# The last stage as one phase: output projection, routing and chosen experts by chunks of 128 tokens

## The chip, the cores and the metric

The kernel runs on one core of one Trainium2 chip. The metric is the device time of one execution in microseconds. The core has five engines, each with its own instruction stream, which wait for one another by semaphores: TensorE (PE in the rows, its weight loads PEld), VectorE (DVE), ScalarE (ACT), GpSimd (POOL) and SyncE (SP, which here only issues DMA transfers). All numbers are float32; a float32 matmul of 128x512 shows as two PE instructions, so "x32" in a row of the trace is 16 matmuls of the code.

## The reference

Four sequences ("batches") of 512 tokens, 512 features wide, pass through four sublayers, each as `x = x + layernorm(f(layernorm(x)))`. The change touches the end of the third (its projection with `Wo` and the two layer norms) and the whole of the fourth:

```python
    return o @ Wo                                    # end of the third sublayer
...
    x0 = x[:, :ROUTE_LEN].reshape(b, -1)             # all 512 x 512 values of a batch
    logits = x0 @ switch_w.T + switch_b              # 8 numbers for a batch
    probs = jax.nn.softmax(logits, axis=-1)
    gate, top_idx = jax.lax.top_k(probs, TOPK)       # 2 experts for a batch
    xh = x.reshape(b, s, H, DH).transpose(0, 2, 1, 3)
    w1s, b1s = (w1[top_idx], b1[top_idx])
    w2s, b2s = (w2[top_idx], b2[top_idx])
    h = jnp.einsum('bhsd,bkfd->bkhsf', xh, w1s) + b1s[:, :, None, None, :]
    h = jax.nn.gelu(h, approximate=False)
    o = jnp.einsum('bkhsf,bkdf->bkhsd', h, w2s) + b2s[:, :, None, None, :]
    o = (o * gate[:, :, None, None, None]).sum(axis=1)
    out = x + o
    return out @ w3.T + b3
```

The experts of a batch can be chosen only when all of its 512 tokens have left the layer norm. The choice concerns that batch alone.

## The kernel before

The kernel is a row of phases; the last two are `phase_delta_out` (tiles named `d_`) and `phase_experts` (tiles named `e_`). The phases ahead of them are the same in both kernels.

`phase_delta_out` works on a batch at a time, four chunks of 128 tokens in each. Per chunk TensorE does 16 matmuls (`outputs`, L2270), one for each head, into one of two PSUM tiles `yo`; ScalarE copies the tile to `y` (L2285), and GpSimd issues the load of the heads for the same chunk of the next batch (L2259). When the four chunks of a batch are there, VectorE normalises them together (`norm_y_vector`, L140 to L154), adds them to `x`, normalises the sum (`norm_x_vector`, L161 to L169), and multiplies the normalised batch with the router's weights for each of the 8 experts (L2312, 2048 columns each, summed by the instruction). ScalarE supplies the inverse square roots by Ln and Exp (L176 to L186), each after a load of its table. TensorE turns the normalised batch (`norm_x_tensor`, L202, 16 transposes) into `XT`, after the outputs of the next batch; for the last batch there is nothing ahead of it.

`phase_experts` begins when `phase_delta_out` has ended on all engines. One matmul sums the routers' parts over the partitions (L2385). VectorE does softmax and the top two for all four batches (L2434 to L2441), picks the chosen experts' weights for all four (`choose`, L2449 and L2451; `choose_bias`, L2456 and L2458), and then a loop runs over the batches: the chosen weights are laid on a block diagonal (L2475), TensorE does hidden layers (L2391) and output layers (L2398) for four groups of features, ScalarE does Gelu between them (L2425), VectorE adds the input (`e_mixed`, L2478), TensorE does the last layer for four chunks (L2412), VectorE adds its bias (L2482), and `norm_y_vector` normalises and adds the batch to `x`, which SP stores (L133).

What sets the order is the order in which each engine's code is written, and the waits; there is no scheduler. The block diagonal of a batch (L2475) stands on VectorE behind the closing norm of the batch ahead.

## Time and profile before

| | us |
|---|---|
| median of 3 runs | 3439.75 (3439.09 to 3444.64) |
| the profiled execution | 3439.55 |
| its span, first to last instruction | 3437.9 |
| first matmul of `phase_delta_out`, from the span's start | 2948.49 |
| PE busy, share of the span | 3019.9, 88% |
| DVE busy | 1859.0, 54% |
| ACT busy | 1200.4, 35% |

In such a profile an engine's busy share is an average over all stages. The two phases of the change are the last 490 us of the span, and are to be read by stretches of time. "PEclk" is the granted TensorE clock, 1.00 for 2.4 GHz and 0.50 for 1.2 GHz. A row of a timeline gives the start, the length, the engine, the line, and in brackets how long the engine was idle before it and what it waited for.

### The profile page before, as it was taken

How to read it: one execution, taken by the hardware profiler on the slowest of the kernel's cores; microseconds unless marked ns; L12 is line 12 of the kernel's file. 1: busy time of each engine (PE TensorE's matmuls, PEld its weight loads, DVE VectorE, ACT ScalarE, POOL GpSimd, SP SyncE). 2: the span in 40 equal slices, each digit the busy share in tenths (PEclk: the TensorE clock that was granted, in tenths of full speed). 3: DMA queues.
4: the chain of work that ended last, by engine and by line, in shares of the span. 5: the costliest groups of instructions: out<-in, count | busy, mean ns of one | idle time of the engine just before them, and what ended most of it. 6: DMA issues, size and time to landing. Idle time of an engine off the chain costs nothing. (4 is left out here: it accounts for less than half of the span.)

```text
span 3437.9 us, 42357 instructions
## 1 busy us (share of the span) xinstructions
PE 3019.9 (88%) x13268; PEld 1724.8 (50%) x13269; DVE 1859.0 (54%) x4426; ACT 1200.4 (35%) x2133; POOL 637.7 (19%) x775
## 2 busy tenths in 40 slices
PE   7899969989996789999999999999999985799276
PEld 3344444435663446665556665566555664344122
DVE  5766730001111867767777677776677764064533
ACT  3554310102211544444544445443454433011121
POOL 1111113001112111222312223122222223000000
PEclk9999969999998889999999999999999997899588
DMA  3001150022123510010000110001100000631111
GB/s 111 25 13 37 61 211 13 24 98 66 62 67 135 224 61 13 14 63 35 17 26 13 63 38 17 23 13 63 38 20 20 13 13 19 250 122 61 43 41 45
DMA packets 67801, 196.98 MB, mean 57 GB/s; under 512 B 10512, under 2 KB 11168, under 8 KB 61216
## 3 DMA queue, kind: packets, MB, share of 16 engines
q1 hardware_dynamic: 46080, 142.06, 11.1%
q0 software_dynamic: 11168, 35.70, 3.1%
q10 hardware_dynamic: 10368, 16.83, 1.3%
q8 instruction: 107, 1.75, 0.2%
q14 instruction: 78, 0.64, 0.1%
HBM read 137.90 MB, written 56.66 MB: 57 GB/s over the span
## 5 line engine op out<-in xcount | busy, mean ns | idle before, releaser
L2061 DVE SCALAR_TENSOR_TENSOR c_conv<-c_ps_pj,c_conv_t,c_conv 128x511 f32<-128x511 f32 (+2 forms) x495 | 368.9, 745 | 35.8 <-ACT c_conv L1910 24.1
L2270 PE MATMUL d_ps_yo<-d_w_o,d_heads 128*128 128x512 f32 x512 | 226.0, 604 | 23.7 <-DMA d_heads<-ot_d 23.7
L1701 PE MATMUL c_ps_pj<-c_xs,c_w_v 128*128 128x512 f32 x480 | 240.8, 626 | 0.0
L1716 PE MATMUL c_ps_pj<-c_w_g,c_xs 128*128 128x512 f32 x512 | 227.6, 592 | 0.0
L1701 PE MATMUL c_ps_pj<-c_xs,c_w_k 128*128 128x512 f32 x480 | 217.7, 597 | 1.9 <-DMA c_xs<-xt_d 1.9
L1701 PE MATMUL c_ps_pj<-c_xs,c_w_q 128*128 128x512 f32 x360 | 166.4, 606 | 25.8 <-DVE c_conv L2061 24.9
L2270 PEld LDWEIGHTS d_ps_yo<-d_w_o,d_heads 128*128 128x128 f32 x512 | 99.1, 194 | 148.9 <-issue 148.9
L1910 ACT ACTIVATE c_conv<-c_ps_pj,c_conv_t 128x512 f32<-128x512 f32 x165 | 127.8, 775 | 116.6 <-PE c_ps_pj L1701 108.8
L1716 PEld LDWEIGHTS c_ps_pj<-c_w_g,c_xs 128*128 128x128 f32 x512 | 94.8, 190 | 107.1 <-issue 107.1
L2082 DVE TENSOR_TENSOR c_block_X<-c_block_X,c_block_t 128x126 f32<-128x126 f32 (+22 forms) x496 | 137.5, 277 | 18.8 <-DVE c_block_t L2078 2.0
L2078 DVE TENSOR_TENSOR c_block_t<-c_block_L,c_block_X 128x126 f32<-128x126 f32 (+22 forms) x496 | 137.0, 276 | 17.5 <-DVE c_block_X L2082 1.7
L1113 DVE TENSOR_TENSOR x_act<-x_hs,x_ps_u 128x352 f32<-128x352 f32 x40 | 20.8, 521 | 227.0 <-ACT x_hs L1098 227.0
L1744 PE MATMUL c_ps_kk<-c_kT 128*128 128x128 f32 x512 | 105.4, 289 | 35.9 <-DVE XT L2153 25.6
L1701 PEld LDWEIGHTS c_ps_pj<-c_xs,c_w_k 128*128 128x128 f32 x480 | 87.1, 191 | 89.3 <-issue 87.2
L1637 POOL TENSOR_TENSOR XT<-XT,c_ln_w 128x512 f32<-128x512 f32 x64 | 81.3, 1270 | 253.4 <-DVE c_block_L L2084 221.2
L966 DVE TENSOR_TENSOR b_act<-b_hs,b_ps_u 128x512 f32<-128x512 f32 (+1 forms) x24 | 16.5, 686 | 206.3 <-PE b_ps_u L858 206.3
L1960 ACT ACTIVATE c_err<-c_negL 32x128 f32<-32x128 f32 x256 | 78.6, 307 | 135.6 <-DVE c_negL L2151 130.9
L1064 PE MATMUL x_ps_g<-b_w_gu,x_xT 128*128 x320 | 122.7, 465 | 1.4 <-ACT x_xT L1089 0.8
L377 PE MATMUL a_ps_pj<-XT,a_w_in 128*128 128x512 f32 x256 | 120.7, 616 | 3.5 <-DVE a_conv L602 2.7
L1701 PEld LDWEIGHTS c_ps_pj<-c_xs,c_w_q 128*128 128x128 f32 x360 | 65.4, 191 | 115.9 <-issue 66.2
L1065 PE MATMUL x_ps_u<-b_w_gu,x_xT 128*128 x320 | 122.0, 463 | 0.0
L357 POOL TENSOR_SCALAR a_skip<-a_xc,a_col_d 128x512 f32<-128x512 f32 x32 | 62.6, 1958 | 315.5 <-ACT a_xc L471 173.0
(377 smaller groups left out, 6116.9 us busy)
## 6 DMA issues: line engine op xcount, KB each, us to landing
c_xs<-xt_d SPq DMA_DIRECT2D x16, 1024.0 KB, 4.9
ot_d<-c_oT ACTq DMA_DIRECT2D x64, 256.0 KB, 2.0
d_heads<-ot_d POOLq DMA_DIRECT2D x16, 1024.0 KB, 7.1
b_w_gu<-in_w_gu SPq DMA_DIRECT2D x8, 1408.0 KB, 25.4
y_slots<-x_y SPq DMA_DIRECT2D x40, 256.0 KB, 2.0
a_x<-in_x SPq DMA_DIRECT2D x8, 1024.0 KB, 6.7
x_w_dn<-in_w_dn SPq DMA_DIRECT2D x8, 768.0 KB, 11.0
x<-a_x SPq DMA_DIRECT2D x4, 1024.0 KB, 4.3
```

The costliest lines, as they stand in the source:

```text
L377: mm = e.matmul(pj[c % 2][:, :], w_in[:, k, c * P:(c + 1) * P], XT[:, b, k, :], start=(k == 0), stop=(k == KD - 1))
L1064: e.matmul(g_ps[par][:, 0:FE], xT[par][:, k, :], w_gu[:, expert, k, 0:FE], start=(k == 0), stop=(k == KD - 1))
L1065: mm = e.matmul(u_ps[par][:, 0:FE], xT[par][:, k, :], w_gu[:, expert, k, FE:2 * FE], start=(k == 0), stop=(k == KD - 1))
L1637: e.tensor_tensor(o[:, c], o[:, c], b, op).then_inc(o_gated, 1)
L1701: mm = e.matmul(bank_of[u][:, :], w["kqv"[u // HG]][:, k, (u % HG) * DH:(u % HG + 1) * DH], xs[xb][:, k, :], start=(k == 0), stop=(k == KD ...
L1716: mm = e.matmul(pj[1 - i % 2][:, :], xs[xb][:, k, i * P:(i + 1) * P], w["g"][:, k, :], start=(k == 0), stop=(k == KD - 1))
L1744: e.matmul(kk[:, h, :], chunk(kT, h, c), chunk(kT, h, c), start=True, stop=True)
L1910: e.activation(conv[:, u % 4, :], bank_of[u][:, :], ACT.Identity, bias=conv_t[buf][:, m, h, TAPS:TAPS + 1], scale=conv_t[buf][:, m, h, TAP ...
L2061: e.scalar_tensor_tensor(oc, bank_of[u][:, 0:SEQ - s], conv_t[buf][:, m, h, TAPS - 1 - s:TAPS - s], oc, ALU.mult, ALU.add).then_inc(conv_s ...
L2078: e.tensor_tensor(t, block_L[:, i + 1:BB, i].unsqueeze(2).to_broadcast([P, n, k]), block_X[:, i, 0:k].unsqueeze(1).to_broadcast([P, n, k]) ...
L2082: e.tensor_tensor(below, below, t, ALU.add).then_inc(sub_step, 1)
L2270: mm = e.matmul(yo[c % 2][:, :], heads[:, c, h, :], w_o[:, h, :], start=(h == 0), stop=(h == NH - 1))
```

## The change

The two phases become one, `phase_out` (all its tiles are named `d_`). The batch is no longer the unit of the norms and the router: every chunk of 128 tokens is normalised as soon as its 16 matmuls are done, by ScalarE straight from PSUM (`scale`), turned one chunk later (`turn`), and multiplied with its 512 columns of the router's weights (`switch_part`, four experts before and four after the second norm of the next chunk). Each batch is routed in the chunks of the next one (`route_front`, `route_back`, `choose`), the experts of batch 0 stand within the matmuls of chunk 14 (`EARLY`), and those of batch 1 behind the last layer of batch 0. The last norm takes its inverse root from VectorE (`last_root`, 16 small steps) in place of Ln and Exp, and ScalarE does its scaling (`scale_z`). All heads are loaded from SP's queue, `w_o` and the router's weights in four parts each. ScalarE's tables are loaded by hand, five changes of table after the first. The loops over batches are written out.

```diff
+ROUTE_FRONT, ROUTE_BACK, ROUTE_STEPS = 4, 20, 35
+Z_STEPS = 16
...
-def phase_delta_out(pr, con, XT, route_part):
+def phase_out(pr, con, XT):
...
+        z = [yn[0], xn[0], yn[1], xn[1]]
...
+        z_ps = [yo[0], yo[1], o_ps[0], o_ps[1]]
...
+            load_heads(0)
+            for g in range(NG):
+                e.dma_start(w_o[:, g * HG:(g + 1) * HG, :], io["w_o"][:, g * HG:(g + 1) * HG, :]).then_inc(wo_loaded[g], 16)
+            load_heads(1)
+            for c in range(TPB):
+                load_x(c)
...
+            load_switch(0)
+            load_switch(1)
+            for n in range(NT):
+                if n + 2 < NT:
+                    load_heads(n + 2)
+                if n == 0:
+                    load_switch(2)
+                    load_switch(3)
+                    e.dma_start(w3[:, :, :], io["w3"]).then_inc(w3_loaded, 16)
+                store_x(n)
+                if n > 0 and n + TPB - 1 < NT:
+                    load_x(n + TPB - 1)
...
+            def outputs(n, of=range(NH)):
+                if of[0] == 0:
+                    e.wait_ge(heads_loaded[n % 2], 16 * (n // 2 + 1))
+                    if n >= 2:
...
+            def turn(n):
+                e.wait_ge(x_normed, n + 1)
+                if n >= 1:
+                    e.wait_ge(xt_done, n)
+                for k in range(KD):
+                    mm = e.transpose(turned[:, k, :], xn[n % 2][:, k * P:(k + 1) * P], con["ident"][:, :])
+                mm.then_inc(turn_ready, 1)
...
+            def output_layer(b, dc):
+                m = KD * b + dc
+                if m >= 2:
+                    e.wait_ge(mixed_done, m - 1)
+                if b > 0 and dc < 2:
+                    e.wait_ge(z_added, TPB * (b - 1) + dc + 3)
...
+            def chosen_experts(b):
                 e.wait_ge(diag_done, 4 * b + 4)
-                hidden_layer(0)
+                e.wait_ge(xt_done, TPB * (b + 1))
...
+            def last_layer(b):
+                e.wait_ge(w3_loaded, 16)
+                for c in range(TPB):
+                    if b == 0 and c < 2:
+                        e.wait_ge(y_normed, NT - 1 + c)
+                    elif c < 2:
+                        e.wait_ge(z_added, TPB * (b - 1) + c + 1)
...
+            for n in range(NT):
+                if n == EARLY:
+                    outputs(n, range(SPLIT))
+                    chosen_experts(0)
+                    outputs(n, range(SPLIT, NH))
+                else:
+                    outputs(n)
+                if n > 0:
+                    turn(n - 1)
+                if n % TPB == 1 and n > TPB:
+                    route_logits(n // TPB - 1)
+            last_layer(0)
+            turn(NT - 1)
+            chosen_experts(1)
+            route_logits(NB - 1)
+            last_layer(1)
+            for b in range(2, NB):
+                chosen_experts(b)
+                last_layer(b)
...
+            def scale(n, dst, src, means, mv, ln_done, ln, rstd, rs, offset, nb, normed):
+                e.wait_ge(means, n + 1)
+                e.activation(ln[:, :], mv[:, 1:2], ACT.Ln, bias=con["eps"][:, :]).then_inc(ln_done, 1)
+                e.wait_ge(ln_done, n + 1)
+                e.activation(rs[:, :], ln[:, :], ACT.Exp, scale=-0.5).then_inc(rstd, 1)
+                e.wait_ge(rstd, n + 1)
+                e.wait_ge(offset, n + 1)
+                e.activation(dst, src, ACT.Identity, bias=nb[:, 0:1], scale=rs[:, 0:1]).then_inc(normed, 1)
...
+            e.preload_act_table_set("natural_log_exp_and_others")
+            for n in range(NT):
+                if n == EARLY:
+                    e.preload_act_table_set("gelu_and_others")
+                    gelus(0)
+                    e.preload_act_table_set("natural_log_exp_and_others")
+                if n > 0:
+                    take_turned(n - 1)
+                scale_y(n)
+                scale_x(n)
+                if n % TPB == 1 and n > TPB:
+                    exponentials(n // TPB - 1)
+            take_turned(NT - 1)
+            e.preload_act_table_set("gelu_and_others")
+            gelus(1)
+            scale_z(0)
+            e.preload_act_table_set("natural_log_exp_and_others")
+            exponentials(NB - 1)
+            e.preload_act_table_set("gelu_and_others")
+            for b in range(2, NB):
+                gelus(b)
+                scale_z(b - 1)
+            scale_z(NB - 1)
...
+                for v in of:
+                    if NE * n + v > 0:
+                        e.wait_ge(switched, NE * n + v)
+                    e.scalar_tensor_tensor(product[:, :], xn[n % 2][:, :], 1.0, switch[:, v, c * DM:(c + 1) * DM],
+                                           ALU.mult, ALU.mult, accum_out=part[b % 2][:, v, c:c + 1]).then_inc(switched, 1)
+            def chunk(n):
+                e.wait_ge(yo_ready, n + 1)
+                statistics(n, yo[n % 2][:, :], y_stats, y_st, y_means, y_mv)
+                if n > 0:
+                    switch_part(n - 1, range(NE // 2))
+                shift(n, y_mv, y_rstd, y_rs, y_offset, y_nb)
+                e.wait_ge(x_loaded[n % TPB], 16 * (n // TPB + 1))
+                e.wait_ge(y_normed, n + 1)
+                xc = x[n % TPB][:, :]
+                e.tensor_tensor(xc, xc, yn[n % 2][:, :], ALU.add).then_inc(x_new, 1)
+                e.wait_ge(x_new, n + 1)
+                statistics(n, xc, x_stats, x_st, x_means, x_mv)
+                if n > 0:
+                    switch_part(n - 1, range(NE // 2, NE))
+                shift(n, x_mv, x_rstd, x_rs, x_offset, x_nb)
...
+            def last_norm(b, c):
+                m = TPB * b + c
+                e.wait_ge(z_ready, m + 1)
+                if b > 0:
+                    e.wait_ge(out_done, m - TPB + 1)
+                e.tensor_tensor(z[c][:, :], z_ps[c][:, :], b3[:, :], ALU.add).then_inc(z_added, 1)
+                e.wait_ge(z_added, m + 1)
+                e.bn_stats(z_st[:, c, :], z[c][:, :]).then_inc(z_stats, 1)
+                e.wait_ge(z_stats, m + 1)
+                e.bn_aggr(z_mv[:, c, :], z_st[:, c, :]).then_inc(z_means, 1)
+            def last_root(b):
+                m = Z_STEPS * b
+                e.wait_ge(z_means, TPB * (b + 1))
+                rstd_vector(e, z_ve[:, :], z_t[:, :], z_rs[:, :], z_mv[:, :, 1], z_step, m)
+                e.wait_ge(z_step, m + Z_STEPS - 1)
+                e.scalar_tensor_tensor(z_nb[:, :], z_mv[:, :, 0], -1.0, z_rs[:, :], ALU.mult, ALU.mult).then_inc(z_step, 1)
+            def finish(b):
+                for c in range(TPB):
+                    m = TPB * b + c
+                    e.wait_ge(x_loaded[c], 16 * (NB + b + 1))
+                    e.wait_ge(z_normed, m + 1)
+                    e.tensor_tensor(x[c][:, :], x[c][:, :], z[c][:, :], ALU.add).then_inc(out_done, 1)
+            for n in range(NT):
+                if n == EARLY:
+                    mix(0)
+                chunk(n)
+                b = n // TPB - 1
+                if b >= 0 and n % TPB == 1:
+                    route_front(b)
+                elif b >= 0 and n % TPB == 2:
+                    route_back(b)
+                elif b >= 0 and n % TPB == 3 and n < NT - 1:
+                    choose(b)
+            e.wait_ge(turn_ready, NT - 1)
+            last_norm(0, 0)
+            last_norm(0, 1)
+            switch_part(NT - 1, range(NE))
+            e.wait_ge(turn_ready, NT)
+            last_norm(0, 2)
+            last_norm(0, 3)
+            last_root(0)
+            choose(NB - 2)
+            mix(1)
+            finish(0)
+            route_front(NB - 1)
+            for b in range(1, NB):
+                for c in range(TPB):
+                    last_norm(b, c)
+                last_root(b)
+                if b == 1:
+                    route_back(NB - 1)
+                if b + 1 < NB:
+                    mix(b + 1)
+                if b == 1:
+                    choose(NB - 1)
+                finish(b)
...
-        phase_delta_out(pr, con, XT, route_part)
-        phase_experts(pr, con, XT, route_part)
+        phase_out(pr, con, XT)```

On TensorE, before, this is what stands between the last outputs and the first expert matmul (`d_ps_tp` the turned chunks, `e_ps_logits` the router's sums, `e_ps_h` the hidden layer):

```order
L202 MATMUL d_ps_tp<-ident,d_yn 128x128 x16
L2219 UNCONDITIONAL_BRANCH
L2382 UNCONDITIONAL_BRANCH
L2385 MATMUL e_ps_logits<-route_part,ones 128x32
L2387 UNCONDITIONAL_BRANCH
L2387 ISA
L2390 ISA
L2391 ISA
L2391 MATMUL e_ps_h<-XT,e_w_diag 128x512
```

Now, on TensorE, from the end of the first batch's experts, which stand within chunk 14 behind 12 of its 16 outputs (`d_ps_o` their output layers, `d_ps_yo` the outputs, L2303 the last layer):

```order
L2278 MATMUL d_ps_o0<-d_hidden,d_w2_diag0 128x512 x2
L2278 MATMUL d_ps_o1<-d_hidden,d_w2_diag0 128x512 x2
L2244 MATMUL d_ps_yo0<-d_w_o,d_heads0 128x512 x4
L2253 MATMUL d_ps_tp<-ident,d_xn1 128x128 x4
L2244 MATMUL d_ps_yo1<-d_w_o,d_heads1 128x512 x16
L2253 MATMUL d_ps_tp<-ident,d_xn0 128x128 x4
L2303 MATMUL d_ps_yo0<-d_w3,d_mixed 128x512 x4
L2303 MATMUL d_ps_yo1<-d_w3,d_mixed 128x512 x4
L2303 MATMUL d_ps_o0<-d_w3,d_mixed 128x512 x4
L2303 MATMUL d_ps_o1<-d_w3,d_mixed 128x512 x4
L2253 MATMUL d_ps_tp<-ident,d_xn1 128x128 x4
L2267 MATMUL d_ps_h0<-XT,d_w1_diag1 128x512
```

The branches between phases are gone, experts and last layer stand among the outputs of the last chunks, and 4 transposes follow every 16 outputs in place of 16 after 64.

On VectorE, before, a batch's norm and the first of its 8 products with the router's weights:

```order
L149 TENSOR_SCALAR d_yn<-d_y,d_mv,d_rs 128x512 x4
L151 ISA
L154 TENSOR_TENSOR d_x<-d_x,d_yn 128x512 x4
L161 BN_STATS d_st<-d_x 128x6 x4
L165 BN_AGGR d_mv<-d_st 128x2 x4
L169 TENSOR_SCALAR d_yn<-d_x,d_mv,d_rs 128x512 x4
L2311 ISA
L2312 SCALAR_TENSOR_TENSOR d_products,d_part<-d_yn,d_switch 128x2048
```

Now, on VectorE, one chunk:

```order
L2398 BN_STATS d_y_st<-d_ps_yo 128x6
L2400 BN_AGGR d_y_mv<-d_y_st 128x2
L2417 SCALAR_TENSOR_TENSOR d_product,d_part<-d_xn,d_switch 128x512 x4
L2404 SCALAR_TENSOR_TENSOR d_y_nb<-d_y_mv,d_y_rs 128x1
L2429 TENSOR_TENSOR d_x<-d_x,d_yn 128x512
L2398 BN_STATS d_x_st<-d_x 128x6
L2400 BN_AGGR d_x_mv<-d_x_st 128x2
L2417 SCALAR_TENSOR_TENSOR d_product,d_part<-d_xn,d_switch 128x512 x4
L2404 SCALAR_TENSOR_TENSOR d_x_nb<-d_x_mv,d_x_rs 128x1
```

The scalings have moved to ScalarE, and the products with the router's weights stand, four at a time, in the gaps in which ScalarE makes a chunk's inverse root.

On VectorE, now, the end of the choice for batch 2 and what follows it, behind chunk 15 (before, the choices of all batches stood ahead of the first block diagonal, L2475):

```order
L2483 TENSOR_TENSOR d_r_score<-d_r_key,d_r_rest 128x8
L2473 TENSOR_TENSOR d_chosen<-d_b,d_r_score 128x8
L2475 TENSOR_REDUCE d_b_sel<-d_chosen 128x1
L2492 TENSOR_TENSOR d_w_diag<-d_same_head,d_w_sel 128x128 x4
L2497 SCALAR_TENSOR_TENSOR d_mixed<-d_ps_o,d_b_sel,XT 128x512 x4
L2523 TENSOR_TENSOR d_x<-d_x,d_yn 128x512
L2523 TENSOR_TENSOR d_x<-d_x,d_xn 128x512
```

The mixing of batch 1 (`d_mixed`), for which TensorE's output layers wait, stands behind the choice for batch 2.

## Rows read from the trace of the kernel before

**Rows 1.** Busy time by stretch: us, PE, PEld, DVE, ACT, POOL, PEclk, DMA share, GB/s

```profile
2948.00:3008.00 60.00, 59.51 (x132) 26.27 (x133) 2.72 (x5) 3.04 (x5) 2.83 (x4) 0.94 0.66 259
...
3128.00:3190.00 62.00, 58.91 (x143) 26.24 (x142) 30.51 (x45) 10.47 (x16) 0.00 (x0) 0.97 0.09 34
3190.00:3220.00 30.00, 4.38 (x16) 2.87 (x16) 24.24 (x33) 8.77 (x13) 0.00 (x0) 0.50 0.09 35
...
3240.00:3271.00 31.00, 11.76 (x23) 4.89 (x24) 17.71 (x59) 5.32 (x8) 0.00 (x0) 0.65 0.00 0
...
3315.00:3355.00 40.00, 27.76 (x55) 11.24 (x54) 12.47 (x27) 8.36 (x11) 0.00 (x0) 0.79 0.16 52
```

**Rows 2.** Timeline of PE: start us, us, engine, line, what, [idle before, releaser]

```profile
2948.49 62.06 PE L2270 MATMUL d_ps_yo<-d_w_o,d_heads 128*128 128x512 f32 x137 [23.67 <-DMA d_heads<-ot_d]
...
3062.94 0.63 PE L202 MATMUL d_ps_tp<-ident,d_yn 128*128 128x128 f32 x4 [0.87 <-ACT XT L193]
...
3203.00 1.12 PE L202 MATMUL d_ps_tp<-ident,d_yn 128*128 128x128 f32 x4 [13.48 <-DVE d_yn L169]
...
3258.48 3.62 PE L2391 MATMUL e_ps_h<-XT,e_w_diag 128*128 x4 [34.12 <-DVE e_w_diag L2475]
...
3300.78 3.78 PE L2391 MATMUL e_ps_h<-XT,e_w_diag 128*128 x4 [10.69 <-DVE e_w_diag L2475]
...
3409.41 14.00 PE L2412 MATMUL e_ps_y<-e_w,e_mixed 128*128 128x512 f32 x32 [0.95 <-DVE e_mixed L2478]
```

**Rows 3.** Timeline of ACT, copies of the first two chunks out of PSUM

```profile
2965.53 0.60 ACT L2285 ACTIVATE d_y<-d_ps_yo 128x512 f32<-128x512 f32 x1 [40.08 <-PE d_ps_yo L2270]
2979.27 0.60 ACT L2285 ACTIVATE d_y<-d_ps_yo 128x512 f32<-128x512 f32 x1 [13.14 <-PE d_ps_yo L2270]
```

**Rows 4.** Timeline of SP, first and last transfer issued in the two phases

```profile
2933.00 0.33 SPq L2242 DMA_DIRECT2D d_w_o<-in_w_o  x1
...
3433.20 0.39 SPq L133 DMA_DIRECT2D out<-e_x  x1
```

**Rows 5.** The page's DMA issues: count, KB each, median us to landing

```profile
ot_d<-c_oT ACTq DMA_DIRECT2D x64, 256.0 KB, 2.0
...
d_w_o<-in_w_o SPq DMA_DIRECT2D x1, 4096.0 KB, 13.5
```

**Rows 6.** Busy time in stretches of 2 us, columns as in rows 1

```profile
2950.00:2952.00 2.00, 2.00 (x3) 0.67 (x2) 0.00 (x0) 0.00 (x0) 0.00 (x0) 0.50 1.03 387
...
3128.00:3130.00 2.00, 2.00 (x3) 0.78 (x3) 0.00 (x0) 1.97 (x3) 0.00 (x0) 0.50 0.00 0
...
3291.00:3293.00 2.00, 0.00 (x0) 0.00 (x0) 2.00 (x4) 0.00 (x0) 0.00 (x0) 0.88 0.00 0
```

**Rows 7.** Groups of instructions from 2930 us on: count, busy us, mean ns, idle before

```profile
L2312 DVE SCALAR_TENSOR_TENSOR d_products<-d_yn,d_switch 128x2048 f32<-128x2048 f32 x32 | 73.3, 2291 | 1.7 <-issue 0.8
...
L2425 ACT ACTIVATE e_hidden<-e_ps_h,e_b_sel 128x512 f32<-128x512 f32 x32 | 21.6, 686 | 26.9 <-PE e_ps_h L2391 26.8
...
L2478 DVE SCALAR_TENSOR_TENSOR e_mixed<-e_ps_o,e_b_sel,XT 128x512 f32<-128x512 f32 x16 | 12.0, 750 | 65.6 <-PE e_ps_o L2398 65.6
...
L140 DVE BATCH_NORM_STATS2 d_st<-d_y 128x6 f32<-128x512 f32 x16 | 10.8, 691 | 161.9 <-ACT d_y L2285 161.2 <-issue 0.7
...
L154 DVE TENSOR_TENSOR d_x<-d_x,d_yn 128x512 f32<-128x512 f32 x16 | 10.0, 683 | 0.0
...
L184 ACT ACT_TABLE_LOAD x4 | 5.1, 1283 | 0.1
...
L2312 DVE DVE_READ_ACCUMULATOR d_products<-d_yn,d_switch 128x1 f32 x32 | 2.6, 81 | 0.0
```

**Rows 8.** Timeline of DVE: an inverse root in 16 steps, first and last; one batch's choice

```profile
2902.02 0.17 DVE L2107 TENSOR_SCALAR c_o_ve<-c_o_mv 128x16 f32<-128x16 f32 x1
...
2905.15 0.17 DVE L2130 SCALAR_TENSOR_TENSOR c_o_nb<-c_o_mv,c_o_rs 128x16 f32<-128x16 f32 x1
...
3236.98 0.42 DVE L2449 TENSOR_TENSOR e_chosen<-e_w,e_r_one 128x256 f32<-128x256 f32 x1
...
3242.01 0.42 DVE L2449 TENSOR_TENSOR e_chosen<-e_w,e_r_one 128x256 f32<-128x256 f32 x1
```

470 lines of the change are left out of this document (195 added, 275 removed).

## The prediction, written before the result was known

> **What bounds the kernel now.** I read the stretches of time first, since only the last 490 us change. While the outputs run, PE is the bound: 58.9 of 62.0 us busy at a clock near 1, VectorE half idle [rows 1]. Then PE is busy for 4.4 of 30 us while VectorE works alone, for 11.8 of 31 us in the stretch of the choice, and for 27.8 of 40 us in an expert batch, at a mean clock of 0.79. The timeline of PE names the waits: 13.48 us for the last batch's norm, 34.12 us for the block diagonal (routing and choice for all batches), and 10.69 us ahead of each later batch, for a diagonal that stands behind the closing norm of the batch ahead [rows 2]. The first matmul comes only at 2948.49, when all of `w_o` has landed and the heads, 15.5 us after SP's first transfer at 2933.00 [rows 2, 4].
>
> Everything that is not PE's own work there is wait. So the new time is: the start of the first matmul, plus PE's own work at the granted clock, plus the waits that are left, plus the tail behind the last matmul.
>
> **The work of PE, which the change does not touch in amount.** The copies of the first two chunks start 13.74 us apart, so 16 outputs take 13.73 and a matmul 0.858 [rows 3]. Sixteen chunks: 16 x 13.73 = 219.7. An expert batch has 8 hidden, 8 output and 16 last-layer matmuls (the 16 last ones take 14.00 with their drain, [rows 2]): 32 x 0.858 = 27.5, four times 109.8. Four transposes take 0.60 to 0.63 [rows 2]; 16 groups, 9.6. Before, three of the four groups of a batch also waited 0.87 for ScalarE's copy; now an output chunk lies between two groups, and that wait goes. The four small router matmuls: 0.3 each, 1.2. The clock starts cold: the first chunk took 2965.53 - 2948.49 = 17.04 in place of 13.73, 3.3 us more [rows 2, 3], and the changed kernel starts as cold. Sum: 219.7 + 109.8 + 9.6 + 1.2 + 3.3 = 343.6.
>
> **The start.** PE now needs the first chunk's heads (1 MiB) and a quarter of `w_o` (1 MiB), issued first on one queue. The engines moved 387 GB/s while loads were outstanding [rows 6]: 2.1 MB take 5.4 us. A transfer of 256 KB lands in 2.0 [rows 5], 0.7 of it moving, so 1.3 is fixed; with SP's 0.33 per issue [rows 4] about 2.1. First matmul at 2933.0 + 5.4 + 2.1 = 2940.5, 8.0 earlier. The bounds: all in one row of 13.5 us for 4 MiB [rows 5] scaled to half, 6.8, gives 2939.8; no gain, 2948.5. The other quarters of `w_o` come every 2.7 us, faster than PE uses them (3.4 us each, 6.9 while cold).
>
> **The queue behind it.** All loads stand on SP's queue in order. Ahead of the heads of chunk 2 are heads 0 and 1, `w_o`, `x` of four chunks, the small tables and half of the router's weights: with themselves 12.5 MiB, 13.1 MB, 33.9 us at 387 GB/s, so about 2969. PE wants them at 2940.5 + 17.0 + 0.6 + 13.7 = 2971.8. Behind come the other half, `w3` and the heads of chunk 3: 18.5 MiB in all, 50.1 us, about 2985.2, wanted at 2986.2. Both are hidden, with 3 and 1 us to spare. I take 0; the other end is a rival below. The Trainium skill ("DMA: Bandwidth & Descriptors", "Where 436 GB/s comes from") puts the limit of one core's loads from device memory at about 358 GB/s. By that the heads of chunk 3 would land at 2989.3 and PE would wait 3 us. The trace has 387 in a stretch of matmuls and loads [rows 6], so the measurement is used.
>
> **VectorE by chunks.** A product with the router's weights took 2291 ns for 2048 columns and 683 for the same kind of two-tensor instruction at 512 [rows 7]; with the read of the accumulator (81, partly covered) I take 0.72 for 512 columns, eight per chunk 5.8. Statistics of the chunk in PSUM and in SBUF 0.69 each, their merging 0.16 each, the add 0.69, two small steps 0.17 each: 2.7. The waits for ScalarE (Ln, Exp, scaling of 512 columns) are mostly filled by the four products; 0.9 stays in front of the add. A chunk costs 9.4 us on VectorE, and PE gives it 14.3. The bounds are 8.5 (no wait left) and 14.3 (from which PE feels it). Routing adds 1, 3.5 and 6 us to three of the four chunks: the choice of one batch took 5.03 [rows 8], with its diagonal 6.0. 15.4 exceeds 14.3 in the chunk of the choice, and the next chunk, with 9.4, takes it up. The turn of a chunk wants its second scaling 14.3 us after its outputs and gets it after about 10. Cost on the path: 0.
>
> The Trainium skill ("VectorE: DVE Perf Modes", "The TRN2 errata — SBUF-src ops pay a fixed extra latency per instruction") speaks against cutting the products up: many small tiles pay a fixed latency each. The two durations above show it: four of 512 columns are 0.44 longer than one of 2048, about 14 us more on VectorE over 32 such cuts. By the rule alone the kernel would be 14 us slower than my sum; by the stretches VectorE has half its time free there [rows 1], and it costs nothing.
>
> ScalarE's tables: each batch of either phase loaded them, at 1.283 us [rows 7], before Ln, Exp and Gelu. Now five changes of table are left; only the one at batch 1's Gelu meets PE.
>
> **The waits left.** Call Y the end of chunk 15's outputs.
> - The second tile of the last layer takes `yo1`, which chunk 15's first scaling must have left. Statistics 0.85, products 2.9, the small step, ScalarE's 0.8 and the hand-over: Y + 4.8. PE is there at Y + 0.6 + 3.4 = Y + 4.0. 0.8 us.
> - Batch 1's first Gelu follows the copy of the turned chunk (0.60 [rows 3]), the table (1.28) and the Gelu (0.69) [rows 7]: 2.7 behind the transposes, PE having 1.7 of work. 1.0 us.
> - Mixing of batch 1. VectorE: chunk 15 until Y + 9.4; two last-layer norms, 1.55 each, Y + 12.6; eight products, Y + 18.3; two norms, Y + 21.5; the root, 16 steps that took 2902.02 to 2905.32 [rows 8], Y + 24.8; the choice for batch 2, Y + 30.8; first mixing 0.75 [rows 7], Y + 31.6. PE: last layer until Y + 15.1, transposes and two hidden layers Y + 17.4, with the Gelu's wait and ten matmuls Y + 27.0, where the third output layer wants that mixing. 4.5 us. Bounds: 0, if the overlaps are better than these sums, and 10.7, the longest wait of this kind before.
> - The clock. In an idle stretch it falls: it was on its way down, 0.88, from 3291 to 3293, in the gap before batch 1's experts [rows 6], whose first two matmuls at 3300.78 then took 3.78 where warm ones take 1.7 [rows 2]; and 0.50 was granted at 3128, right behind transposes with gaps of 0.87 [rows 2, 6]. The cold start cost 3.3. I take 3.3 behind the wait of 4.5; the bounds are 0 and twice that.
> Sum 0.8 + 1.0 + 4.5 + 3.3 = 9.6. For batches 2 and 3 the diagonal is made during the matmuls of the batch ahead (VectorE's chain of about 9 us from the last layer to the mixing, against 10.3 of PE work), so no wait: that is where 3 x 10.69 and their cold clock go.
>
> **The tail.** Behind the last matmul: bias 0.69, statistics 0.69, merging 0.16, root 3.3, four scalings by ScalarE 0.75 each, the last add 0.7, the store of 256 KB 0.4 + 2.0, hand-overs 0.4: 11.3. Before, from 3423.4 (3409.41 + 14.00) to 3437.9: 14.5 [rows 2]. The four stores begin 3 us ahead of the end and no longer wait for one another.
>
> **Sum.** 2940.5 + 343.6 + 9.6 + 11.3 = 3305.0 of span. The execution before took 3439.55 for a span of 3437.9, 1.65 more, and lies 0.2 under the median: 3307. That is 133 us less than 3439.75.
>
> **Rivals.**
> A, the queue: the many rows of 2 KB of the cut transfers move at less than 387 GB/s, or SP, waiting for `x` of a chunk to be stored, issues heads late. At 300 GB/s 18.5 MiB take 64.7 us: heads of chunk 2 at 2979 (7 us late), of chunk 3 at 3000, 7 more. PE loses 14, and with the clock that falls in such gaps 20: 3327. For it: the spare time is only 1 us. Against: the heads, in rows of the same kind, moved at full rate in the 387 stretch.
> B, the norm chain: if a chunk's chain through VectorE and ScalarE takes over 14.3 us and not 10, PE waits at each turn. At 16 us: 15 x 1.7 = 26, less the wait for mixing unchanged: 3333. For it: ten hand-overs in a chain, each a guess of under 0.1. Against: 4 us of room.
> C, the change does less than it says: the diagonals of batches 2 and 3 come late after all, because VectorE also adds and finishes the batch ahead. Two waits of 10.7 with 3.3 of cold clock each: 28 more, 3335. Against: the order puts mixing and choice ahead of finishing.
> D, slower than before: VectorE becomes the bound, if a product's price is one of instruction and not of columns. At 2.37 us (2291 and 81 ns [rows 7]) for each of eight, a chunk is 22.6, 8.3 over PE's 14.3; over 15 chunks 125, with routing then on the path (10.5 for each of three batches, 31) 156 in all: 3463. It passes 3440 from about 2.2 us on. For it only that this width with an accumulator is nowhere in the trace; against, the add at 512 columns with 683.
>
> **Chances.** Forecast 0.72, with its own range 3297 to 3316; A 0.13; B 0.06; C 0.05; D 0.02; 0.02 for other things, half of them faster. Faster by over 0.2% (7 us, about what a measurement of this kernel tells from none) is all but D and half a point: 0.97; same 0.01; slower 0.02. The range for 8 in 10 goes from 3296 (no wait for mixing and no cold clock behind it, 7.8 less, and 3 of hand-overs) to 3328 (A).
>
> **What would show it.** First matmul at 2940 to 2942. Chunks 14.3 us apart on PE, with no DMA wait at chunks 2 and 3 (A), no wait for `x_normed` ahead of transposes (B). Products at 0.7 us (D). One wait of 3 to 6 us at the third output layer of batch 1, with PEclk at 0.5 behind it. PE without a gap over 1 us in the last two batches (C). Less than 12 us behind the last matmul. If the chunks stand 15 us or more apart, the prediction is wrong whatever the total.

## The result, and the profile after

The changed kernel took 3307.36 us in the median of 4 runs (3299.81 to 3307.89), the kernel before 3441.66 (3439.09 to 3444.64) beside it: a ratio of 0.9604, 95% interval 0.9588 to 0.9621. The prediction was 3307, range 3296 to 3328. The profiled execution took 3307.89 for a span of 3306.2 us.

That the number was met has a lucky part. The phases ahead of the change are the same code in both kernels, but SP's first transfer of the last stage came at 2937.01 in this execution and at 2933.00 in the one before. From here on "the stage" is the time from that transfer to the end of the span: 504.9 us before (3437.9 - 2933.0), 369.2 after (3306.2 - 2937.0). The prediction, taken the same way, was 372.0. So the stage came out 2.8 shorter than predicted, and the phases ahead 4.0 longer.

Busy time by stretch in the changed kernel (columns as in [rows 1]); the first three rows answer to [rows 6], the later ones to [rows 1]:

```profile
2941.00:2945.00 4.00, 0.00 (x0) 0.00 (x0) 0.00 (x0) 0.00 (x0) 0.00 (x0) 0.50 1.01 407
...
2949.00:2955.00 6.00, 6.00 (x13) 2.67 (x12) 0.00 (x0) 0.00 (x0) 0.00 (x0) 0.82 1.01 401
2957.00:2987.00 30.00, 30.00 (x74) 13.52 (x73) 10.74 (x30) 5.68 (x13) 0.00 (x0) 1.00 1.05 386
3128.00:3190.00 62.00, 62.00 (x158) 28.06 (x158) 35.78 (x113) 18.59 (x34) 0.00 (x0) 1.00 0.16 52
3190.00:3220.00 30.00, 24.81 (x60) 10.50 (x58) 27.13 (x87) 12.85 (x21) 0.00 (x0) 1.00 0.15 44
3240.00:3271.00 31.00, 31.00 (x73) 13.32 (x72) 24.69 (x84) 10.37 (x15) 0.00 (x0) 1.00 0.17 51
```

PE is busy throughout the chunks (62.00 of 62) and through a batch of experts (31.00 of 31, where it had 11.76 before and 27.76 of 40 in an expert batch). VectorE does more in the chunks, 35.8 of 62 against 30.5, and is the busier one only in the 30 us behind chunk 15. In the three rows of the first 50 us, loads moved 386 to 407 GB/s.

PE's timeline, answering to [rows 2]; all its waits in the stage are here, but for one of some 0.3 us ahead of chunk 3, which shows only in the times: 0.64 us from the start of the transposes (2990.06) to the outputs (2990.70), where other chunks have 0.43, and 0.1 within the chunk.

```profile
2945.57 30.48 PE L2244 MATMUL d_ps_yo<-d_w_o,d_heads 128*128 128x512 f32 x64 [17.34 <-DMA d_w_o<-in_w_o]
...
2990.06 0.60 PE L2253 MATMUL d_ps_tp<-ident,d_xn 128*128 128x128 f32 x4
2990.70 14.00 PE L2244 MATMUL d_ps_yo<-d_w_o,d_heads 128*128 128x512 f32 x32
...
3004.97 13.90 PE L2244 MATMUL d_ps_yo<-d_w_o,d_heads 128*128 128x512 f32 x32
...
3194.14 3.70 PE L2303 MATMUL d_ps_yo<-d_w,d_mixed 128*128 128x512 f32 x8 [0.91 <-ACT d_yn L2340]
...
3207.83 1.98 PE L2267 MATMUL d_ps_h<-XT,d_w_diag 128*128 128x512 f32 x4 [0.97 <-ACT d_hidden L2364]
...
3220.36 5.40 PE L2278 MATMUL d_ps_o<-d_hidden,d_w_diag 128*128 128x512 f32 x8 [3.67 <-DVE d_mixed L2497]
...
3287.99 7.03 PE L2303 MATMUL d_ps_o<-d_w,d_mixed 128*128 128x512 f32 x16
```

The 13.48, the 34.12 and the three waits of 10.69 are gone. Of the new waits the longest is 3.67, and its eight matmuls take 5.40 where such eight take 3.60 elsewhere. A chunk with its transposes takes 14.17 (14.32 where the router's small matmul stands in it; 14.27 for chunk 3, 2990.70 to 3004.97), and no transposes wait.

The stage splits the same way in both kernels. Before, PE's waits inside it sum to 110.2: nine of 0.87 and three of 0.78 for the turned chunk, 13.48 for the norm, 14.03 ahead of the logits, 34.12, the three of 10.69, and 6.4 in small ones. "Work" is what is left when start, waits and tail are taken off, so it holds the time lost to a low clock.

| us | before | after | predicted |
|---|---|---|---|
| first transfer to first matmul | 15.5 | 8.6 | 7.5 |
| PE's waits | 110.2 | 5.8 | 6.3 |
| PE's work | 364.7 | 343.6 | 346.9 |
| behind the last matmul | 14.5 | 11.2 | 11.3 |
| stage | 504.9 | 369.2 | 372.0 |

Of 135.7 us saved, 104.4 are waits and 21.1 are work, which did not change in amount. Most of that is the clock of an engine that no longer stops (granted clock 1.00 in the last three rows above, 0.97, 0.50 and 0.65 in the same stretches of [rows 1]): an estimate from the lengths of the same groups of matmuls gives 18 of the 21.

Groups of instructions of the changed stage, answering to [rows 7] (count, busy us, mean ns, idle before):

```profile
L2417 DVE SCALAR_TENSOR_TENSOR d_product<-d_xn,d_switch 128x512 f32<-128x512 f32 x128 | 88.0, 687 | 3.4
...
L2398 DVE BATCH_NORM_STATS2 d_y_st<-d_ps_yo 128x6 f32<-128x512 f32 x16 | 11.2, 698 | 107.3 <-PE d_ps_yo L2244 107.3
...
L2417 DVE DVE_READ_ACCUMULATOR d_product<-d_xn,d_switch 128x1 f32 x128 | 10.5, 82 | 0.0
```

A product of 512 columns took 0.687, so rival D is out, and VectorE waited 107 us for PE over 16 chunks: it still has room. One chunk without routing, from its first statistics to its last small step, takes VectorE 9.3 us (2990.26 to 2999.54), where the prediction had 9.4:

```profile
2990.26 0.70 DVE L2398 BATCH_NORM_STATS2 d_y_st<-d_ps_yo 128x6 f32<-128x512 f32 x1 [4.91 <-PE d_ps_yo L2244]
...
2999.39 0.15 DVE L2404 SCALAR_TENSOR_TENSOR d_x_nb<-d_x_mv,d_x_rs 128x1 f32<-128x1 f32 x1
```

The cut costs VectorE 98.5 us for 128 products against 75.9 for 32 wide ones [rows 7], 22.6 more and not the 14 foreseen, of which 7.9 are the reads of the accumulator (10.5 for 2.6), one for each product. It was hidden all the same.

SP's timeline, answering to [rows 4], and one page row, answering to [rows 5]:

```profile
2937.01 0.38 SPq L2165 DMA_DIRECT2D d_heads<-ot_d  x1
...
2962.35 0.39 SPq L2165 DMA_DIRECT2D d_heads<-ot_d  x1
2962.78 7.09 SPq L2179 DMA_DIRECT2D d_switch<-in_switch_w  x2
2969.91 5.28 SPq L2212 DMA_DIRECT2D d_w<-in_w  x1
...
2976.08 0.39 SPq L2165 DMA_DIRECT2D d_heads<-ot_d  x1
```
```profile
d_heads<-ot_d SPq DMA_DIRECT2D x16, 1024.0 KB, 5.4
```

The heads of chunk 3 are issued at 2976.08 and used at 2990.70: 14.6 us on the way, with the router's second half and `w3` ahead of them, where a chunk's heads take 5.4 in the median. They could not be issued sooner. There are two buffers for heads, so SP waits for the outputs of chunk 1 (`yo_ready`), which end as the transposes at 2975.89 begin. The DMA engines were busy all this time (columns as above, from the first transfer to the first output of chunk 3; share 1.00, 376 GB/s):

```profile
2937.01:2990.71 53.70, 45.10 (x105) 20.16 (x105) 11.19 (x31) 6.98 (x15) 0.90 (x13) 0.87 1.00 376
```

VectorE behind chunk 15, answering to [rows 8]: first and last step of the root, first step of the choice, the diagonal, the first mixing, and the last add of the kernel:

```profile
3210.63 0.17 DVE L112 TENSOR_SCALAR d_z_ve<-d_z_mv 128x4 f32<-128x4 f32 x1
...
3213.63 0.16 DVE L2516 SCALAR_TENSOR_TENSOR d_z_nb<-d_z_mv,d_z_rs 128x4 f32<-128x4 f32 x1
3213.71 0.42 DVE L2466 TENSOR_TENSOR d_chosen<-d_w,d_r_one 128x256 f32<-128x256 f32 x1
...
3218.75 0.90 DVE L2492 TENSOR_TENSOR d_w_diag<-d_same_head,d_w_sel 128x128 f32<-128x128 f32 x4
3219.56 1.40 DVE L2497 SCALAR_TENSOR_TENSOR d_mixed<-d_ps_o,d_b_sel,XT 128x512 f32<-128x512 f32 x2
...
3302.96 0.69 DVE L2523 TENSOR_TENSOR d_x<-d_x,d_xn 128x512 f32<-128x512 f32 x1
```

Chunk 15's outputs ended at 3189.2, the Y of the prediction. The mixing starts at Y + 30.4 (predicted: done at Y + 31.6), directly behind 5.9 us of choice and diagonal.

### The profile page after: what moved, and what is told of

Read it like the earlier page. It is cut to its first block and busy times, and to the rows that moved or that the text cites. A ratio compares the mean times of both kernels' runs of the same rounds, so it can differ in the third digit from the quotient of the medians.

```text
span 3306.2 us, 42307 instructions
## 1 busy us (share of the span) xinstructions
PE 2999.0 (91%) x13274; PEld 1718.7 (52%) x13275; DVE 1879.8 (57%) x4723; ACT 1208.8 (37%) x2186; POOL 623.5 (19%) x759
## 5 line engine op out<-in xcount | busy, mean ns | idle before, releaser
L2244 PE MATMUL d_ps_yo<-d_w_o,d_heads 128*128 128x512 f32 x512 | 225.6, 599 | 17.4 <-DMA d_w_o<-in_w_o 17.3
L1793 ACT ACTIVATE c_conv<-c_ps_pj,c_conv_t 128x512 f32<-128x512 f32 x165 | 127.8, 774 | 114.4 <-PE c_ps_pj L1584 107.3
L2244 PEld LDWEIGHTS d_ps_yo<-d_w_o,d_heads 128*128 128x128 f32 x512 | 97.3, 192 | 134.9 <-issue 134.6
L1627 PEld LDWEIGHTS c_ps_kk<-c_kT 128*128 128x128 f32 x512 | 84.5, 200 | 72.5 <-DVE XT L2036 43.8
## 6 DMA issues: line engine op xcount, KB each, us to landing
c_xs<-xt_d SPq DMA_DIRECT2D x16, 1024.0 KB, 4.9
ot_d<-c_oT ACTq DMA_DIRECT2D x64, 256.0 KB, 2.0
d_heads<-ot_d SPq DMA_DIRECT2D x16, 1024.0 KB, 5.4
y_slots<-x_y SPq DMA_DIRECT2D x40, 256.0 KB, 2.0
a_x<-in_x SPq DMA_DIRECT2D x8, 1024.0 KB, 6.5
d_x<-x SPq DMA_DIRECT2D x32, 256.0 KB, 2.9
```

The lines of the kernel that those rows point to most:

```text
L1627: e.matmul(kk[:, h, :], chunk(kT, h, c), chunk(kT, h, c), start=True, stop=True)
L1793: e.activation(conv[:, u % 4, :], bank_of[u][:, :], ACT.Identity, bias=conv_t[buf][:, m, h, TAPS:TAPS + 1], scale=conv_t[buf][:, m, h, TAP ...
L2244: mm = e.matmul(yo[n % 2][:, :], heads[n % 2][:, h, :], w_o[:, h, :], start=(h == 0), stop=(h == NH - 1))
```

## The experiments

Each run is compared by the stage in its profile, because the phases ahead, identical in all kernels, moved SP's first transfer over a range of 12 us (2930.4 to 2942.6 in the 14 profiles), more than most of the effects. The ratios to the kernel before are of whole runs; the changed kernel's is 0.960. Its stage took 369.2 and 369.6 us in two profiles; differences are given from 369.4.

| run | median us | ratio, 95% interval | first transfer | span | stage |
|---|---|---|---|---|---|
| changed kernel | 3307.36 | 0.9604 (0.9588-0.9621) | 2937.0 | 3306.2 | 369.2 |
| after_again | 3305.14 | 0.9605 (0.9587-0.9623) | 2930.4 | 3300.0 | 369.6 |
| mix_first | 3299.77 | 0.9583 (0.9567-0.9599) | 2934.0 | 3297.6 | 363.6 |
| warm | 3306.27 | 0.9599 (0.9581-0.9617) | 2942.6 | 3311.8 | 369.2 |
| start | 3302.19 | 0.9594 (0.9575-0.9614) | 2934.1 | 3301.0 | 366.9 |
| warm_queue | 3299.79 | 0.9586 (0.9570-0.9603) | 2937.5 | 3303.5 | 366.0 |
| heads_behind | 3318.79 | 0.9642 (0.9626-0.9658) | 2936.7 | 3318.5 | 381.8 |
| products2 | 3311.07 | 0.9617 (0.9596-0.9637) | 2939.4 | 3312.4 | 373.0 |
| products8 | 3344.45 | 0.9715 (0.9696-0.9733) | 2934.6 | 3342.3 | 407.7 |
| route_late | 3320.06 | 0.9645 (0.9629-0.9661) | 2936.1 | 3320.6 | 384.5 |
| before_diag | 3418.49 | 0.9928 (0.9910-0.9946) | 2940.2 | 3423.9 | 483.7 |
| before_diag_root | 3400.22 | 0.9867 (0.9848-0.9885) | 2939.2 | 3402.8 | 463.6 |
| best | 3295.14 | 0.9574 (0.9558-0.9591) | 2932.0 | 3290.7 | 358.7 |

**after_again**: no edit.

> The changed kernel once more, as the measure for the other runs on this chip. The last stage, from SP's first transfer in it to the end of the span, took 369.2 us in the first profile; if the 4 us by which the phases ahead were longer there are variation between executions, the stage is again within 0.5 us of 369.2 while the phases ahead lie anywhere between 2933 and 2937. If instead the changed kernel slows the phases ahead (other memory addresses, other code), they end at 2937 again, and the total is 3307.

The stage was 369.6, with the first transfer at 2930.4, earlier than the 2933 to 2937 expected. So the 4 us of the first profile are variation between executions, not a cost of the change. The two profiles of the changed kernel show where it comes from. They differ by 6.6 us at the first transfer of the stage, and by 4.4 already at the first store of the first sublayer (236.77 and 232.36 us). From 60 to 180 us the granted clock averaged 0.90 in one and 0.94 in the other. The same eight matmuls of the first sublayer took 5.19 us there behind a wait of 2.45, and 3.70 behind one of 1.51.

**mix_first**, the largest wait left:

```
-            choose(NB - 2)
             mix(1)
+            choose(NB - 2)
```

> VectorE mixes batch 1 before it makes the choice for batch 2. Theory 1, that of the prediction: the 3.67 us for which TensorE waits at the third output layer of batch 1 are there only because the choice (5.9 us) stands ahead of the mixing on VectorE, and the clock falls in that wait (1.8 us more for the eight matmuls behind it). The root ends at 3213.8, mixing then starts 5.9 earlier, before TensorE wants it: the wait goes, the stage takes 369.2 - 5.4 = 363.8 us (363 to 365.5). Rival: the wait is only handed on, since the choice now falls into the last layer of batch 1 and the diagonal of batch 2 or the closing norm of batch 1 comes late: a wait of 3 to 6 us ahead of batch 2's experts or its third output layer, and the stage is within 1 us of 369.2.

Stage 363.6. PE's row at that place no longer waits:

```profile
3213.60 3.60 PE L2278 MATMUL d_ps_o<-d_hidden,d_w_diag 128*128 128x512 f32 x8
```

Nothing later waits in its place: PE's timeline has no gap from here to its last matmul. Theory 1 holds, wait and clock together (369.4 - 363.6 = 5.8 against 3.67 + 1.80; the 0.3 that is left is within the differences at chunk 3, where this run waited 1.50).

**before_diag**, one part of the change alone, on the kernel before:

```
-                        e.tensor_tensor(diag[:, k], heads4, ...)        # in the loop, ahead of mixing
+                        e.tensor_tensor(diag[b % 2][:, k], heads4, ...) # in diagonal(b)
...
                 (mixing of b)
+                if b + 1 < NB:
+                    diagonal(b + 1)
```

> The kernel before with one part of the change alone: two block diagonals in turn, the next batch's made behind the mixing of this one and ahead of its last layer and closing norm. Theory 1: the three waits of 10.69 us ahead of later batches are there only because the diagonal stands behind the norm; they go. What is late next is mixing: VectorE leaves the closing norm about 10.7 us behind the last matmul, TensorE wants the first mixing after 12 matmuls, 10.3 us, and 0.75 is the mixing itself: a wait of 1 to 2 us is left per batch. Saved 3 x (10.7 - 1.5) = 27.6 and 1 to 2 us of cold clock each: the stage takes 504.9 - 31 = 474 us (470 to 479), the total about 3409. Rival: the norm holds up the mixing for as long as it held up the diagonal (the wait moves whole to the third output layer, 8 to 10 us): saved under 8 us in all.

Stage 483.7, a gain of 21.2 where 31 were expected: neither theory. The diagonal's wait is gone, but another took its place. PE, and below it ScalarE, at the change from batch 0 to 1:

```profile
3297.42 1.88 PE L2391 MATMUL e_ps_h<-XT,e_w_diag 128*128 128x512 f32 x4
3304.92 3.78 PE L2391 MATMUL e_ps_h<-XT,e_w_diag 128*128 128x512 f32 x4 [5.62 <-ACT e_hidden L2425]
```
```profile
3301.05 0.30 ACT L176 ACTIVATE e_ln<-e_mv,eps 128x4 f32<-128x4 f32 x1 [19.62 <-DVE e_mv L144]
3301.37 1.28 ACT L178 ACT_TABLE_LOAD   x1
3302.66 0.20 ACT L178 ACTIVATE e_rs<-e_ln 128x4 f32<-128x4 f32 x1
3302.88 1.28 ACT L2425 ACT_TABLE_LOAD   x1
3304.18 1.26 ACT L2425 ACTIVATE e_hidden<-e_ps_h,e_b_sel 128x512 f32<-128x512 f32 x2
```

The Gelus of the next batch stand on ScalarE behind the closing norm's Ln and Exp, which wait for VectorE's statistics, and behind two tables. So the second half of the gain belongs to another part of the change: the root on VectorE.

**before_diag_root** adds that part:

```
-                norm_y_scalar(e, n, b, con["eps"][:, :])
+    rstd_vector(e, ve, t, n.rs1[:, :], n.mv1[:, :, 1], step, 15 * r)
```

> The kernel of the run before_diag (the kernel before with two block diagonals, the next made ahead of the closing norm) with one more part of the change: the root of the closing norm is computed by VectorE in 15 small steps, and no longer by ScalarE's Ln and Exp with their two tables. In before_diag each of the three later batches waited 5.62 us at its second hidden layer, because its Gelus stood behind Ln, Exp and 2.6 us of table loads on ScalarE, and the clock fell there. Theory 1: that wait goes with the root; what is late next is mixing: statistics end 3.6 us behind the last matmul, root 3.3, scaling and adding 4.3, mixing 0.75, together 12 against the 10.3 us of TensorE's twelve matmuls: a wait of 1.5 to 2.5 us at the third output layer. Saved 3 x (5.6 + 2 of cold clock - 2) = 17 and up to 2 more or less for the clock behind the new wait; the last batch's tail is 1.4 longer. Stage 483.7 - 17 + 1.4 = 468 us (464 to 473). Rival (the Gelu wait was the switch of tables for Gelu alone, or the wait moves whole to mixing, 5 us and its cold clock): the stage is within 4 us of 483.7.

Stage 463.6, another 20.1, more than the 15.7 expected and just outside the range of 464 to 473. The wait fell from 5.62 to 1.36 with a warm clock behind it, and the wait of 1.5 to 2.5 expected for the mixing did not come:

```profile
3299.50 1.98 PE L2399 MATMUL e_ps_h<-XT,e_w_diag 128*128 128x512 f32 x4 [1.36 <-ACT e_hidden L2433]
```

The two parts together give 41.3 of the 135.7; the three waits of 10.69 alone were 32.1.

**route_late**, the routing out of the chunks:

```
-                if b >= 0 and n % TPB == 1:
-                    route_front(b)
...
+            for b in range(2):
+                route_front(b)
+                route_back(b)
+                choose(b)
+            mix(0)
+            route_front(2)
+            route_back(2)
```

The new lines stand behind chunk 15, and so do the experts of batch 0 on TensorE and ScalarE.

> The changed kernel with the routing of batches 0 to 2 no longer in the next batch's chunks: it comes behind chunk 15, and so do the experts of batch 0. Theory 1 (routing in the chunks is hidden, and undone costs one batch's routing on the path; the others are covered by the experts of the batch ahead): TensorE waits about 1 + 3.5 + 6 = 10.5 us with 1 to 2 of hand-overs ahead of the first experts, some 2 of cold clock, and 1 to 3 for mixing batch 0 behind the routing of batch 1: stage 369.2 + 16 = 385 (381 to 392). Rival (every batch's routing comes onto the path): three times 10.5 and their cold clocks, stage 400 or more. Rival (chunks get shorter without the routing, as they had been bound by VectorE): chunks under 14.0 us apart, and the stage grows by under 8.

Stage 384.5, 15.1 more:

```profile
3184.46 0.61 PE L2260 MATMUL d_ps_logits<-d_part,ones 128*128 128x32 f32 x2 [9.87 <-ACT d_r_score L2352]
3193.40 5.46 PE L2267 MATMUL d_ps_h<-XT,d_w_diag 128*128 128x512 f32 x8 [8.33 <-DVE d_w_diag L2487]
```

The chunks stayed 14.17 apart without the routing, so in them it cost nothing. Undone, one batch's routing shows: 9.87 (chunk 15's own chain on VectorE comes first) + 8.33, 1.7 of low clock behind it (5.46 for 3.78), less the wait of 0.91, less 2.25 at the mixing of batch 1 (1.42 there) and its 1.8 of clock: 15.0. The rival of three exposed routings is out: the later ones are covered by experts.

**products2** and **products8**, VectorE's room. The edit, with EXTRA 2 or 8:

```
+                    if v < EXTRA:
+                        e.scalar_tensor_tensor(product2[:, :], xn[n % 2][:, :], 1.0, switch[...],
+                                               ALU.mult, ALU.mult, accum_out=spare[:, :]).then_inc(again, 1)
```

> Two of the eight products of a chunk are done twice: 1.45 us more on VectorE per chunk, 10.9 against TensorE's 14.2; four chunks with a batch's routing 54.1 against 56.7. Theory 1: the chunks stay 14.2 apart; behind chunk 15 VectorE reaches the mixing of batch 1 1.45 us later for its products of chunk 15, and the wait there is 5.1 and not 3.7: the stage is 369.4 + 1.5 = 370.9 us (370.5 to 372.5). Rival (the chunk of the choice, 15.4 + 1.5 us, already stops TensorE): one wait of 1 to 3 us in each of three batches, and the stage grows by 4 or more.

> Each of the eight products of a chunk with the router's weights is done twice, the second result unused: 8 x (0.687 + 0.04) = 5.8 us more on VectorE per chunk. Theory 1 (a chunk costs 9.4 us on VectorE and TensorE gives it 14.2): it now costs 15.2, and four chunks with the routing of a batch 71.3 against 56.7 of TensorE. The slack absorbed all of it before; now VectorE is the bound. The chunks of the first batch lie 15.2 apart, those of the three later ones 17.8 on average less the spare time of the chunk with the early experts (27 us): 4 + 14.6 + 14.6 + about 0 = 33 us more by chunk 15, and some 5 behind it: stage 369.2 + 38 = 407 (400 to 415). Rival (VectorE in truth had more room or waits that the added products fill, so that a chunk costs 13 to 14): the added work is mostly hidden, and the stage grows by under 15 us. Rival (products cost more with two streams in SBUF while ScalarE reads it): chunks over 17 us apart from the start, and over 60 more.

products8: stage 407.7, and theory 1 had 407, but its parts did not come so. By the end of chunk 15 the run was 27 us behind the changed kernel and not 33, and it lost another 11 behind it and not 5. A chunk took VectorE 14.2 us (3032.28 to 3046.48) and not 15.2, since a doubled product adds 0.62 to the chunk and not 0.73. That just equals PE's 14.2; but the chain of a chunk's norm has ScalarE's scaling behind it as well, and so it ends later than PE wants the turn. PE's transposes now wait for that chain (10 waits, 18.8 us in all), and the chunk behind a long one runs on a lower clock:

```profile
3099.27 0.66 PE L2257 MATMUL d_ps_tp<-ident,d_xn 128*128 128x128 f32 x4 [3.89 <-ACT d_xn L2344]
...
3100.00 15.58 PE L2248 MATMUL d_ps_yo<-d_w_o,d_heads 128*128 128x512 f32 x32
```

Four chunks take 67.2 us here (3032.85 to 3100.00) for 56.9 in the changed kernel; the forecast had 71.3.

products2: the chunks stayed 14.2 apart, as expected, but the stage grew by 3.6, not 1.5, outside its range (370.5 to 372.5). The place is the second tile of the last layer, which waits for a scaling that stands behind the first half of the products; I had put the delay at the mixing alone:

```profile
3199.15 5.40 PE L2307 MATMUL d_ps_yo<-d_w,d_mixed 128*128 128x512 f32 x8 [2.20 <-ACT d_yn L2344]
```

That is 1.3 more wait and 1.7 for the clock behind it; a new wait of 1.00 at batch 0's first Gelu and 0.4 less at the mixing make up the rest.

**heads_behind**, the queue of loads made longer:

```
             load_switch(1)
+            load_switch(2)
+            load_switch(3)
+            e.dma_start(w3[:, :, :], io["w3"]).then_inc(w3_loaded, 16)
             for n in range(NT):
```

> The second half of the router's weights and w3 (5 MiB) are issued ahead of the heads of chunk 2 and not behind them. Theory 1 (the prediction's queue: all loads move one after another at about 400 GB/s, and the heads of chunk 2 have 3 us to spare): they land 13.1 us later, TensorE waits 10 us (8 to 12) for them, with 1 to 3 of cold clock; the heads of chunk 3 are no longer late. Stage 369.2 + 11 = 380 (377 to 384). Rival (transfers share the engines and small waits, not the order, set the landing): the wait is under 5 us and falls on chunk 3. Rival (SP's own issuing, slow while its queue is full, sets it): the wait is 15 us or more, as each further issue costs SP 4 to 7 us.

```profile
2986.35 16.52 PE L2243 MATMUL d_ps_yo<-d_w_o,d_heads 128*128 128x512 f32 x32 [10.50 <-DMA d_heads<-ot_d]
```

Stage 381.8, as theory 1 had it: the wait is 10.50, and its chunk takes 2.6 more than 13.90. If the added loads take the 13.1 us of the expectation, the heads of chunk 2 had 2.6 to spare, which agrees with the prediction's 3. Both rivals, under 5 us or over 15, are out: what stands ahead on the queue counts.

**warm**, five matmuls on constants ahead of the first:

```
+            for i in range(WARM):
+                e.matmul(turned[...], con["ident"][:, :], XT[:, 0, 0, :], start=True, stop=True)
```

> Five matmuls of 512 columns on constants, whose results are overwritten, run on TensorE while the first heads and the first quarter of w_o are on their way. Theory 1: the first chunk takes 3 us longer than a warm one only because the granted clock is 0.50 when it starts; with the engine busy ahead of it the clock is up, chunks 0 and 1 take 27.7 us and not 30.5, and the stage is 2.5 to 3 us shorter than 369.2. Rival 1: the first chunk is held up by the arrival of the later quarters of w_o (PE would wait for DMA between its groups, 0.5 to 1 us each), and the stage is shorter by less than 1 us. Rival 2: a faster TensorE wants the heads of chunks 2 and 3 3 us earlier, and these then come late, since they came with less than 1 us to spare: two waits on DMA that give back most of it, and the stage is shorter by under 1 us.

```profile
2942.63 6.74 PE L2309 MATMUL d_ps_tp<-XT,ident 128*128 128x512 f32 x10 [8.22 <-PEq L74]
2950.83 27.70 PE L2245 MATMUL d_ps_yo<-d_w_o,d_heads 128*128 128x512 f32 x64 [1.46 <-DMA d_w_o<-in_w_o]
...
2996.30 14.00 PE L2245 MATMUL d_ps_yo<-d_w_o,d_heads 128*128 128x512 f32 x32 [2.79 <-DMA d_heads<-ot_d]
```

The clock was up and the first two chunks took 27.70, not 29.2 to 30.5; yet the stage is 369.2. That is rival 2, with one wait on DMA, at chunk 3, and none at chunk 2. Chunk 3 starts 53.7 us behind SP's first transfer, as in the changed kernel (53.7, and 54.1 the second time), whatever the first chunks took.

**start**, the first heads in four parts, each with its quarter of `w_o`:

```
-            load_heads(0)
             for g in range(NG):
+                e.dma_start(heads[0][:, g * HG:(g + 1) * HG, :], io["ot_d"][g, 0, 0]).then_inc(first_loaded[g], 16)
```

> The first heads come in four transfers of 256 KB, each ahead of its quarter of w_o, so that the first matmul needs 1.25 MiB and not 2 MiB. Theory 1: the first matmul comes 0.75 MiB / 0.4 MB per us = 2.0 us earlier, 6.5 us after SP's first issue; but chunk 3 waits for the queue and starts at 53.7 to 54.1 as before, so the stage stays at 369.4 (369.0 to 369.8). Rival (the path runs through TensorE from the first matmul): the stage is 1.5 to 2 us shorter.

```profile
2939.99 30.42 PE L2247 MATMUL d_ps_yo<-d_w_o,d_heads 128*128 128x512 f32 x64 [14.04 <-DMA d_w_o<-in_w_o]
...
2987.29 14.00 PE L2247 MATMUL d_ps_yo<-d_w_o,d_heads 128*128 128x512 f32 x32 [2.27 <-DMA d_heads<-ot_d]
...
3216.93 3.70 PE L2281 MATMUL d_ps_o<-d_hidden,d_w_diag 128*128 128x512 f32 x8 [3.65 <-DVE d_mixed L2500]
```

The first matmul came 5.9 us behind the first transfer and chunk 3 still at 53.2: of 2.7 us, 0.5 to 0.9 was left. The stage, 366.9, is 2.5 shorter all the same, outside the range of theory 1 (369.0 to 369.8) and beyond the rival's 1.5 to 2. The last row says why: the mixing wait is as long as ever, but the eight matmuls behind it took 3.70, not 5.40. Nothing in the edit touches that place 230 us later (see the last section), so I do not count this 1.7 for it.

**warm_queue**, warm with a shorter queue:

```
-            for dst, name in ((w1, "w1"), (w2, "w2"), (b1, "b1"), (b2, "b2")):
-            ...
             for n in range(NT):
                 if n + 2 < NT:
                     load_heads(n + 2)
-                if n == 0:
-                    load_switch(2)
-                    load_switch(3)
-                    e.dma_start(w3[:, :, :], io["w3"]).then_inc(w3_loaded, 16)
+                if n < 2:
+                    load_switch(n + 2)
+                if n == 2:
+                    for dst, name in ((w1, "w1"), (w2, "w2"), (b1, "b1"), (b2, "b2")):
+                    ...
+                    e.dma_start(w3[:, :, :], io["w3"]).then_inc(w3_loaded, 16)
```

> The five early matmuls of the run warm, and with them a shorter queue: the small tables (w1, w2, b1, b2, switch_b, b3) and w3 are issued behind the heads of chunk 4, a quarter of the router's weights behind those of chunk 2 and another behind those of chunk 3. In all six kernels with the changed order the matmuls of chunk 3 start 53.7 to 54.1 us after SP's first issue, whether the first two chunks took 27.7, 29.2 or 30.5. Theory 1 (until chunk 3 it is the queue of loads that sets the time, so the cold clock cost nothing there): with the queue shortened the warm clock shows: chunk 3 starts at 8.3 + 27.7 + 0.6 + 13.7 + 0.6 = 50.9 us, and the stage takes 369.4 - 2.9 = 366.5 us (366 to 367.5). Rival (the time from a chunk's end to its next heads is set by SP, which waits for x of a chunk to be stored, and not by what moves ahead): chunk 3 starts at 53 or later again, and the stage is within 0.8 of 369.4.

```profile
2946.02 27.70 PE L2245 MATMUL d_ps_yo<-d_w_o,d_heads 128*128 128x512 f32 x64 [1.69 <-DMA d_w_o<-in_w_o]
...
2988.17 13.90 PE L2245 MATMUL d_ps_yo<-d_w_o,d_heads 128*128 128x512 f32 x32
```

Chunk 3 started at 50.6 without a wait, and the stage is 366.0, 3.4 shorter. The same five matmuls gave nothing behind a full queue. How the 3.4 divides is not shown, since the shorter queue was not run without them. Against `after_again` the first two chunks are 1.45 shorter (27.70 for 29.15) and the wait of 1.89 at chunk 3 is gone; with PE's cold start left in, the shorter queue might have given that 1.89 alone.

**best**, the four edits together:

> Four things together: mixing ahead of the choice (as mix_first), the five early matmuls, the shorter queue (as warm_queue), and the first heads in four transfers (as start). If the gains add up where the queue no longer binds: 5.6 for the mixing, 2.9 for the clock, 1.5 to 2.0 for the earlier first matmul: stage 369.4 - 10.2 = 359.2 us (358.5 to 361). If the queue binds again for an earlier first matmul (heads of chunk 1 or 2 late), 1 to 2 of it are lost: 361 to 363.

Stage 358.7, 10.7 shorter than the changed kernel's 369.4, where 10.2 were expected. The whole kernel took 3295.14, a ratio of 0.9574 to the kernel before. The changed kernel has 0.9605 in a comparison of its own; the intervals of the two overlap by 0.0004, but all four runs of `best` (3292.49 to 3295.58) lie below all eight of the changed kernel (3299.81 to 3310.63), and the stage in the profiles says the same. It beats both kernels.

## Why the prediction was right

It summed what PE must do and what it must wait for. Both sums held in the main; one path, the queue of loads up to chunk 3, was wrong in kind and came out right by luck:

- **PE's work**: 343.6 + 3.3 predicted, 343.6 measured. Too high were the transposes, of which four add 0.44 to a chunk and not 0.60 (2.6 over 16 chunks), since their end overlaps the next chunk; the clock behind the mixing wait, 1.8 and not 3.3; and the cold start, 2.8 in the first profile and 1.5 in the second (30.48 and 29.15 against 27.70) and not 3.3. Against that stand some 1.5 us of small steps wherever the work changes or resumes, which were not in the sum.
- **Start**: 8.6 for 7.5 (8.2 to 8.6 over the profiles with this order of loads). The rate was at least as assumed (407 GB/s from 2941 to 2945), so the part put at 2.1 beside the moving of 2 MiB was 2.8 to 3.2. The term was sized too small; whether the rest is fixed time, or time shared with the transfers issued behind, is open. `start` had 0.75 MiB less ahead of it and came 2.3 to 2.7 us earlier, where the bytes alone make 2.0.
- **The queue**: 3 us to spare for chunk 2 agrees with `heads_behind` (2.6). 1 us for chunk 3 does not: it waited 0.3 and 1.9 in the two profiles, and 1.5 to 1.8 in `mix_first`, `route_late` and `products2`. By the prediction's own signs a DMA wait at chunk 3 speaks for rival A, and this is the step that was wrong in kind. Those heads started PE 53.7 us behind the first transfer, which the prediction put at 52.2 (2985.2 - 2933.0). The loads ahead and their rate were right. What it left out are the stores of `x3`: two of 256 KB were issued before chunk 3 started, which at 387 GB/s is an estimated 1.4 us. SP's slow issuing is not shown to cost anything beside that, since the DMA engines were busy all the time. With no spare time, the queue and not PE set the time until chunk 3. So the start and the cold clock of the sum were terms of a path that was not the longer one: `warm` took the cold clock away and gained nothing. The total came out right because the predicted path through PE to chunk 3, 53.2 us, was nearly as long as the queue's 53.7. Rival A, at 300 GB/s and 20 us, named the mechanism but not its size. The Trainium skill ("DMA: Bandwidth & Descriptors", "Where 436 GB/s comes from") gives a limit of about 358 GB/s for loads from device memory; the trace has 386 to 407 while loads were outstanding, and the measurement decides. The measured 0.3 and 1.9 lie between that rule's 3 and my 0, though not for its rate.
- **VectorE by chunks**: cost on the path 0, and it was 0; a chunk took VectorE 9.3 us for the 9.4 predicted. `products2` and `products8` show the room: 1.45 us more per chunk leave the chunks 14.2 apart, 4.9 more do not. That the total of `products8` was forecast to 0.7 us is in part luck, since the 27 and 11 of which it is made were put at 33 and 5. The Trainium skill ("VectorE: DVE Perf Modes", "The TRN2 errata — SBUF-src ops pay a fixed extra latency per instruction") says that many small tiles pay the fixed latency each. The trace agrees: 22.6 us more on VectorE. They were worth nothing to the time while PE was the bound.
- **Routing in the chunks**: 0 predicted; `route_late` had the same chunk time without it.
- **The waits left**: 0.8, 1.0 and 4.5 predicted, 0.91, 0.97 and 3.67 measured, at the three places named. The 4.5 was 0.8 too long: VectorE's first mixing ends at Y + 31.1 and not 31.6, and PE wants it at Y + 27.5 and not 27.0. `mix_first` shows that its cause was the one given.
- **Batches 2 and 3**: no gap, as predicted; but the reason given, the diagonal made early, was half of it. In the kernel before, `before_diag` left a wait of 5.62 us per batch at the Gelus, and `before_diag_root` brought it to 1.36. The prediction counted that root as a cost of 3.3 us and did not see what it took off ScalarE. That the wait is 0 in the changed kernel goes with its order on ScalarE, where the Gelus of the next batch also stand ahead of the scalings of the closing norm; that part was not run by itself.
- **Tail**: 11.3, measured 11.2.

Not tried: the merging of norms and products into the chunks by itself. The waits that it took away, 13.48, 14.03 and most of 34.12, are the larger part of the 104.4 us of waits that went. That they went with it is read from the two traces and argued from the order of the code; of the runs only `route_late` undoes a part of it (15.1 us).

## What to carry to other kernels

Count an engine's own work and its waits apart and sum both; then do the same for the queue of loads, as a second path, because a gain on the engine (an earlier start, a warm clock) is worth nothing until the transfer that it next needs has room. Count the stores on that queue too, and note from when each load may be issued at all. When a wait is removed, go down every engine that feeds the waiting one and ask what stands ahead of its next instruction: taking the diagonal out of the norm's shadow exposed Gelus behind the same norm on another engine. And where one engine does a chain for another, put the step that is wanted first in front: one exchanged pair of lines gave 5.8 us.

## What the runs showed of the hardware that was not expected

The clock behind a short wait is not settled by the wait. The same wait of 3.65 to 3.67 us at the same place was followed by eight matmuls in 5.40 in the changed kernel, in `after_again`, `warm`, `warm_queue` and `heads_behind`, and in 3.70 in `start`. The granted clock in stretches of 2 us, first of the changed kernel, then of `start`:

```profile
3219.00:3221.00 2.00, 0.64 (x2) 0.34 (x3) 1.96 (x6) 1.98 (x3) 0.00 (x0) 0.96 0.00 0
3221.00:3223.00 2.00, 2.00 (x4) 0.97 (x3) 0.00 (x0) 0.52 (x1) 0.00 (x0) 0.50 0.00 0
```
```profile
3215.00:3217.00 2.00, 0.07 (x1) 0.08 (x1) 1.93 (x8) 1.98 (x4) 0.00 (x0) 1.00 0.00 0
3217.00:3219.00 2.00, 2.00 (x5) 0.98 (x6) 0.58 (x2) 1.11 (x1) 0.00 (x0) 1.00 0.00 0
```

In the first the clock went to half (1.2 of 2.4 GHz) when the matmuls had resumed, in the second not at all. A wait of 2.20 in `products2` was followed by the low clock too, one of 1.36 in `before_diag_root` was not, and neither were those of 2.79 in `warm` and 2.27 in `start` ahead of chunk 3 (14.00 us each). So the length of a wait of 2 to 4 us did not settle it.

Issuing a transfer took SP 0.33 to 0.44 us when little was outstanding, and 3.5 and 5.3 (two of the router's quarters in 7.09, `w3` in 5.28) when an estimated 3 to 5 MiB were outstanding, by what had been issued and what the engines had moved. SP was so itself late with the first store of `x3` (ready at 2965.7, issued at 2975.24). In `warm` it was also 3 us late with the heads of chunk 3, issued at 2981.44 when chunk 1 had ended at 2978.4; in the changed kernel's first profile it was just in time.

Identical code ahead of the stage took 2930.4 to 2942.6 us in 14 profiled executions. Between the two profiles of the changed kernel, part of the difference is the same uncertain clock behind short waits (see `after_again`). An effect under 5 us is only to be read in the stage, and there too 1.7 us can come from the clock alone.
